# A selective scan with channels on partitions and its states in turn

## The chip, the cores and the metric

The kernel runs on one core of a Trainium2 chip. The metric is the device time in microseconds of one execution: the median of three runs before the change is 840.94 us (840.87 to 842.92). Engines are named as in the profile: PE (TensorE, matrix products), PEld (its weight loads), DVE (VectorE), ACT (ScalarE), POOL (GpSimd) and SP (SyncE, which issues all DMAs).

## What is computed

32 images are cut into 36 patches each and run through one tower layer: patch embedding, layer norm, a gated block with a selective scan, a feed-forward block, layer norm, and a mixture of 16 experts of which 4 are used per token. The change concerns the scan:

```python
dt_in, Bm, Cm = jnp.split(xdbl, [DT_RANK, DT_RANK + D_STATE], axis=-1)
dt = jax.nn.softplus(jnp.einsum('blr,dr->bld', dt_in, W_dt) + b_dt)
A = -jnp.exp(A_log)
A_bar = jnp.exp(dt[..., None] * A)
Bx = (dt * z)[..., None] * Bm[:, :, None, :]
_, h = jax.lax.associative_scan(comb, (A_bar, Bx), axis=1)   # h = A_bar * h + Bx
y = jnp.einsum('blds,bls->bld', h, Cm) + D_skip * z
```

d runs over 384 inner channels, s over 16 states, l over the 36 tokens of an image; A_log differs from channel to channel and from state to state. B and C (Bm, Cm) have one value per token and state, for all channels.

## The kernel before

The work is cut into 4 chunks of 8 images, T = 288 tokens in a row on the free axis. One list (`schedule()`, the ORDER) fixes the program order of every engine. Each chunk has phase A (embedding to feed-forward) and phase B (the experts). Phase A of chunk 0 runs alone, together with a prologue (`split_w1`, 16 times) that splits the expert weights into two float32r parts and stores them to DRAM. Then a loop of three passes runs phase A of chunk c interleaved with phase B of chunk c-1, and phase B of the last chunk ends the program. How many pieces of phase B stand ahead of a step of phase A is a table (PIECES_BEFORE for expert up projections, DOWNS_BEFORE for down projections, SPLIT_BEFORE for the prologue's splits).

In the scan a partition holds one pair of channel and state: 8 channels times 16 states make a group, 48 groups cover 384 channels, and a step takes two groups, 576 columns; 24 steps per chunk, 8 for each of three blocks of 128 channels. The values of a group come from the [channel, token] tiles through PE, as a float32r product with a 0/1 matrix (`pick_group`) that repeats each channel over 16 partitions. For that dt and u = dt*z are split into high and low halves first (`split`: ACT copies, DVE or POOL subtractions into `dt_rows`, `u_rows`). A step (`expand_u`, `expand_dt`, `drive`, `decay_step`, `advance`, `collect`) is:

- PE: two products of u_rows into the PSUM banks pb 0 and 1 (after DVE has read the last pair), two of dt_rows into pa 0 and 1 (after ACT has read them)
- DVE: `b_x` = B * u, 576 columns, out of PSUM (line 1013); ACT: `a_bar` = exp(decay * dt), two halves out of PSUM
- DVE: `tensor_tensor_scan` of `a_bar` and `b_x`, both in SBUF, into `state`, 576 columns (line 1022)
- POOL: `read` = state * C, 576 columns (line 1262); DVE does the last of the chunk (line 1029)
- PE: two f32 products of `read` with `sum_channel` (128 rows, 32 columns each) that add the 16 states of each channel in pa bank 2; after 8 steps DVE makes y (line 1037)

`state`, `a_bar` and `read` have two buffers, `b_x` three. The softplus of blocks 1 and 2 is done inside the scan: ACT `square`, then at steps 4 and 12 five dependent DVE instructions (`log1p`, lines 983 and 987), then `split` at steps 6 and 14. Fifteen down projections stand inside the scan of each pass of the loop, and no up projection does. Five splits of the prologue stand in the scan of chunk 0 or at its end, seven behind it.

## Time and profile before

The profiled execution took 842.2 us, of which the span of the core's instructions is 840.4 us.

| | |
|---|---|
| median of three runs | 840.94 us |
| profiled execution | 842.2 us |
| its span | 840.4 us |
| PE busy | 642.1 us (76%) |
| DVE busy | 557.6 us (66%) |
| POOL busy | 314.2 us (37%) |
| ACT busy | 268.3 us (32%) |
| mean granted TensorE clock | 0.83 |

The span is a start of 52.6 us, a scan of 86.0 us, and a tail of chunk 0 of 55.7 us; then three passes of the loop, each with a scan of about 79 us and about 112 us of other work; and a last stretch of experts. "Start to start" below is the difference of two rows' start times. An arrow gives the engine that ended a wait.

### The profile page before, as it was taken

The page shows a single profiled execution, that of the slowest core. Times are in us where ns is not written, and L with a number is a line of the kernel's source. Part 1 is how long each engine was busy: PE and PEld are TensorE (multiplying, and loading weights), DVE is VectorE, ACT ScalarE, POOL GpSimd, SP SyncE. Part 2 cuts the span into 40 slices and gives each one's busy share as a digit, 9 for nine tenths or more (in the row PEclk, how much of TensorE's full clock was granted, in tenths as well). Part 3 has the DMA queues.
Part 4 walks back from the last instruction along what each step waited for, and adds up shares of the span by engine and source line. Part 5 has one row for each costly group of instructions (what it writes and reads, how often), then busy time and mean ns, then how long its engine had stood idle before and what let it go on. Part 6 is the DMA issues. An engine that isn't in the chain of part 4 may idle for free.

```text
span 840.4 us, 10439 instructions
## 1 busy us (share of the span) xinstructions
PE 642.1 (76%) x2988; PEld 434.8 (52%) x2988; DVE 557.6 (66%) x944; ACT 268.3 (32%) x617; POOL 314.2 (37%) x283
## 2 busy tenths in 40 slices
PE   5636466768877758988877758989967758987986
PEld 4423233547643437856743427767743426856664
DVE  3268975244798885555698895554698894555464
ACT  1363341213634322212543322212544322222231
POOL 2535774532236542121236552131136552122222
PEclk8756766759976789979967689989977699986999
DMA  9830202553300003132300003132200003131340
GB/s 292 268 133 1 92 24 73 176 200 136 113 1 2 0 1 114 57 124 99 113 0 1 0 0 113 57 124 100 79 33 1 0 0 110 59 123 56 114 161 20
DMA packets 15138, 66.55 MB, mean 79 GB/s; under 512 B 2096, under 2 KB 7648, under 8 KB 9840
## 3 DMA queue, kind: packets, MB, share of 16 engines
q1 hardware_dynamic: 15088, 66.04, 23.0%
q14 instruction: 38, 0.31, 0.1%
q8 instruction: 12, 0.20, 0.1%
HBM read 55.71 MB, written 10.32 MB: 79 GB/s over the span
## 4 chain that ended last, share of the span: by engine, by line
PE 40%; issue 23%; POOL 15%; DVE 14%; ACT 5%; SPq 1%; DMA 1%; POOLq 1%; DVEq 0%; ACTq 0%
PE pa L487 21%; PE pb L487 19%; POOL read L1262 5%; POOL scratch L1275 4%; DVE state L1022 3%; POOL root L1206 2%; DVE dt L983 1%; ACT scratch L765 1%; DVE hid L1168 1%; DVE scratch L1151 1%; POOL u_rows L1243 1%; POOL u L1236 1%; POOL w L1222 1%; DVE scratch L1159 1%; DVE b_x L1013 1%
## 5 line engine op out<-in xcount | busy, mean ns | idle before, releaser
L1275 POOL TENSOR_TENSOR scratch<-scratch 128x288 f32<-128x288 f32 x96 | 77.4, 806 | 290.5 <-DVE scratch L1159 290.5
L1262 POOL TENSOR_TENSOR read<-state,c_all 128x576 f32<-128x576 f32 x92 | 135.9, 1481 | 118.0 <-DVE state L1022 116.2
L1022 DVE TENSOR_TENSOR_SCAN state<-a_bar,b_x 128x576 f32<-128x576 f32 x96 | 172.0, 1795 | 5.3 <-POOL read L1262 3.5
L487 PE MATMUL pb<-t_high,w 128*128 128x288 f32 x576 | 154.6, 333 | 9.4 <-DVE scratch L1143 6.3
L765 ACT ACTIVATE a_bar<-pa,decay 128x280 f32<-128x280 f32 x192 | 84.4, 490 | 155.0 <-PE pa L487 82.0
L487 PE MATMUL pb<-u_rows,pick_group 128*128 128x288 f32 x192 | 69.6, 454 | 73.4 <-DVE b_x L1013 57.2
L487 PEld LDWEIGHTS pb<-t_high,w 128*128 128x128 f32 x576 | 104.0, 198 | 30.8 <-DVE scratch L1143 11.3
L487 PE MATMUL pb<-hid,w 128*64 128x288 f32 (+1 forms) x384 | 106.5, 480 | 17.4 <-DVE hid L1168 17.4
L487 PE MATMUL pa<-read,sum_channel 128*32 128x288 f32 x384 | 85.3, 544 | 36.3 <-POOL read L1262 24.8
L487 PE MATMUL pb<-t_low,w 128*128 128x288 f32 x384 | 111.0, 303 | 0.0
L765 ACT ACTIVATE scratch<-pb,vec 128x288 f32<-128x288 f32 x96 | 48.0, 500 | 179.9 <-PE pb L487 179.8
L487 PEld LDWEIGHTS pb<-u_rows,pick_group 128*128 128x128 f32 x192 | 40.8, 255 | 124.5 <-DVE b_x L1013 90.8
L1013 DVE TENSOR_TENSOR b_x<-b_all,pb 128x576 f32<-128x576 f32 x96 | 70.9, 739 | 23.8 <-PE pb L487 23.5
L487 PEld LDWEIGHTS pb<-hid,w 128*64 128x64 f32 (+1 forms) x384 | 46.3, 179 | 61.1 <-issue 35.8
L487 PEld LDWEIGHTS pb<-t_low,w 128*128 128x128 f32 x384 | 75.3, 196 | 0.0
L1143 DVE TENSOR_SCALAR scratch<-pb,vec 128x288 f32<-128x288 f32 x96 | 49.4, 514 | 37.2 <-PE pb L487 36.6
L487 PE MATMUL pa<-dt_rows,pick_group 128*128 128x288 f32 x192 | 56.6, 385 | 7.2 <-ACT a_bar L765 7.2
L1168 DVE TENSOR_TENSOR hid<-scratch,pb 128x288 f32<-128x288 f32 x96 | 43.2, 450 | 22.1 <-POOL scratch L1275 22.1
L487 PEld LDWEIGHTS pa<-dt_rows,pick_group 128*128 128x128 f32 x192 | 43.6, 260 | 10.7 <-ACT a_bar L765 10.2
L487 PEld LDWEIGHTS pa<-read,sum_channel 128*32 128x32 f32 x384 | 16.2, 125 | 62.3 <-POOL read L1262 33.3
L765 ACT ACTIVATE scratch<-scratch 128x288 f32<-128x288 f32 x96 | 41.8, 436 | 14.4 <-DVE scratch L1143 14.3
L1159 DVE SCALAR_TENSOR_TENSOR scratch<-scratch 128x288 f32<-128x288 f32 x96 | 43.7, 456 | 0.9
(146 smaller groups left out, 859.5 us busy)
## 6 DMA issues: line engine op xcount, KB each, us to landing
w<-w_store SPq DMA_DIRECT2D x32, 1152.0 KB, 5.1
w_store<-w SPq DMA_DIRECT2D x8, 1152.0 KB, 5.0
scratch<-expert_w SPq DMA_DIRECT2D x16, 384.0 KB, 5.6
x_patch<-patches SPq DMA_DIRECT2D x4, 864.0 KB, 4.6
w<-expert_w SPq DMA_DIRECT2D x1, 2304.0 KB, 13.5
x_patch<-patches SPq DMA_DIRECT2D x3, 288.0 KB, 4.2
w_embed<-embed_w SPq DMA_DIRECT2D x3, 256.0 KB, 3.7
out_main<-result SPq DMA_DIRECT2D x4, 144.0 KB, 2.2
```

Of the source, the lines that this page charges most:

```text
L487: return nc.tensor.matmul(out, lhsT, rhs, start=start, stop=stop)
L765: return nc.scalar.activation(out, in_, func, **kw)
L983: dve.scalar_tensor_tensor(dt[:, j, :], factors[:, k, :], rest, product, ALU.add, ALU.mult).then_inc(poly.sem, 1)
L1013: dve.tensor_tensor(b_x[:, i % 3, :].rearrange("p (k t) -> p k t", k=2), twice(b_all[:, :]), pb[:, 0:2, 0:T], ALU.mult).then_inc(bx_ready. ...
L1022: dve.tensor_tensor_scan(state[:, i % 2, :], a_bar[:, i % 2, :], b_x[:, i % 3, :], 0.0, ALU.mult, ALU.add).then_inc(scanned.sem, 1)
L1143: dve.tensor_scalar(g_min[un % 2], pb[:, GATE, 0:T], col("b1_gate", un), LIMIT, ALU.add, ALU.min)\
L1151: dve.tensor_scalar(l_clip[un % 2], l_raw[un % 2], 1.0 + LIMIT, 1.0 - LIMIT, ALU.min, ALU.max)\
L1159: dve.scalar_tensor_tensor(g_act, g_tanh, 1.0, g_min[un % 2], ALU.add, ALU.mult)\
L1168: dve.tensor_tensor(hid[:, un % HID_TILES, :], glu, pb[:, WEIGHT, 0:T], ALU.mult)\
L1206: pool.tensor_tensor(root[:, 1, :], root[:, 0, :], minus_half[:, :], ALU.pow)\
L1262: pool.tensor_tensor(read[:, i % 2, :].rearrange("p (k t) -> p k t", k=2), state[:, i % 2, :].rearrange("p (k t) -> p k t", k=2), twice(c_ ...
L1275: pool.tensor_tensor(glu, g_act, l_clip[un % 2], ALU.mult).then_inc(glu_ready.sem, 1)
```

## The change

In the new scan a partition is a channel. A half step g handles one block of 128 channels and one state, 288 columns; two halves are a step, so there are again 24 steps and 48 halves per chunk.

- B is not kept: for each half PE spreads one row of `bc_parts` over all 128 partitions into pa bank 0 or 1 (`spread`, one float32r product whose weights are one column of `pick_state` repeated), as soon as the scan two halves earlier is done. DVE multiplies it by u in place in PSUM (`fill`), and the scan reads a_bar from SBUF and b_x from PSUM (`advance`).
- C is spread once per chunk: 16 products and 16 ACT copies into `c_all` (16 x 288 columns), in `broadcast`, which now follows `log1p` of block 0.
- a_bar comes from `dt` in SBUF directly, with a decay per partition; no splits, no `dt_rows`, `u_rows`, `pick_group`. POOL makes u of blocks 1 and 2 (`drive_u`).
- The states are added by two f32 products of `read` with the 128x128 identity into pa bank 2, over a whole block.
- `decay` needs another layout: it is turned by a DMA of single elements into DRAM (`decay_rows`) and loaded from there; ACT waits for this load first of all. The loads of group_pick and channel_sum are gone.
- Buffers: a_bar 4 halves, state 3, read 3. The three ACT copies of pick_unit in chunk 0 become one, at `outproj`. Ten prologue splits stand in the scan of chunk 0, three behind it.
- Down projections stand one ahead of each collect; as before fifteen of them come to stand in the scan. Eleven expert units stand ahead of the scan, as before.

```diff
+HALVES = 2 * SCAN_STEPS
+A_SLOTS, STATE_SLOTS, READ_SLOTS = 4, 3, 3
...
-    pre += [("xproj", 0), ("delta", 0), ("broadcast", 0)]
-    pre += [("square", k) for k in range(FACTORS)] + [("log1p", 0), ("split", 0)]
+    pre += [("xproj", 0), ("delta", 0)] + [("square", k) for k in range(FACTORS)]
+    pre += [("log1p", 0), ("broadcast", 0)]
...
-                scan.append(("split", j + 1))
-        scan += [("scan", i), ("decay", i)]
-        if i >= 1:
-            scan.append(("advance", i - 1))
-        if i >= 3:
-            scan.append(("collect", i - 3))
-    scan += [("collect", SCAN_STEPS - 3), ("advance", SCAN_STEPS - 1), ("collect", SCAN_STEPS - 2),
-             ("collect", SCAN_STEPS - 1)]
+                scan.append(("drive_u", j + 1))
+        scan.append(("decay", i))
+        for g in (2 * i, 2 * i + 1):
+            scan += [("fill", g), ("advance", g)]
+        scan.append(("read", i))
+        if i >= 2:
+            scan.append(("collect", i - 2))
+    scan += [("collect", SCAN_STEPS - 2), ("collect", SCAN_STEPS - 1)]
...
-DOWNS_BEFORE = {("scan", 3): 1, ("scan", 4): 2, ("scan", 5): 1, ("scan", 6): 1, ("scan", 8): 2,
-                ("scan", 9): 1, ("scan", 12): 1, ("scan", 13): 3, ("scan", 17): 1, ("scan", 18): 1,
-                ("scan", 19): 1, ("scan", 20): 2, ("scan", 23): 1}
...
-SPLIT_BEFORE = [("inproj", 1), ("inproj", 2), ("xproj", 0), ("delta", 0), ("scan", 1), ("scan", 11),
-                ("scan", 13), ("scan", 19), ("outproj", 0), ("scale2", 0), ("ffn", 0), ("ffn", 1),
-                ("down", 0), ("center3", 0), ("variance3", 0), ("scale3", 0)]
...
+DOWNS_BEFORE = {("collect", i): 1 for i in range(1, 22)}
+SPLIT_BEFORE = [("inproj", 1), ("inproj", 2), ("xproj", 0), *(("decay", 2 * n + 2) for n in range(10)),
+                ("variance2", 0), ("ffn", 0), ("ffn", 1)]
...
+            sp.dma_start(decay_rows, decay_log.rearrange("p g -> g p"), allow_slow_non_contiguous=True)\
+                .then_inc(decay_turned.sem, 16)
...
+            sp.wait_ge(decay_turned.sem, 16)
+            sp.dma_start(decay[:, :, :], decay_rows.rearrange("(j a) (b n) -> (a b) j n", j=NJ, n=STATES))\
+                .then_inc(load_decay.sem, 16)
...
+            def spread(bank, which, n):
+                pick = pick_state[:, which, n:n + 1].to_broadcast([P, P])
+                return mm(pa[:, bank, 0:T], pick, bc_parts[:, :], True, True)
...
-                for k in range(2):
-                    pe.wait_ge(v_max.sem, v_max.at(c, k + 1))
-                    mm(pa[:, 1 + k, 0:T], pick_state[:, k, :], bc_parts[:, :], True, True).then_inc(pe_bc.sem, 1)
...
-            def expand_u(c, i):
-                j = i // STEPS_PER_BLOCK
-                if i:
-                    pe.wait_ge(bx_ready.sem, bx_ready.at(c, i))
...
-                for k in range(2):
-                    _, q, b = scan_slot(i, k)
-                    last = mm(pb[:, k, 0:T], pick_group[:, 4 * (b % 2) + q, :], u_rows[:, j, b // 2, :], True, True)
-                last.then_inc(pe_u_all.sem, 1)
-            def expand_dt(c, i):
...
-                    mm(pa[:, k, 0:T], pick_group[:, 4 * (b % 2) + q, :], dt_rows[:, j, b // 2, :],
-                       True, True).then_inc(pe_dt_all.sem, 1)
+                for n in range(STATES):
+                    if n < NJ:
+                        pe.wait_ge(v_max.sem, v_max.at(c, n + 1))
+                    else:
+                        pe.wait_ge(c_ready.sem, c_ready.at(c, n - NJ + 1))
+                    spread((n + 1) % NJ, 1, n).then_inc(pe_c.sem, 1)
+            def fill(c, g):
+                if g < 2:
+                    pe.wait_ge(c_ready.sem, c_ready.at(c, STATES))
+                else:
+                    pe.wait_ge(scanned.sem, scanned.at(c, g - 1))
+                spread(g % 2, 0, g % STATES).then_inc(pe_b.sem, 1)
...
                 for k in range(2):
-                    _, q, b = scan_slot(i, k)
-                    last = mm(pa[32 * b:32 * b + 32, 2, 0:T], sum_channel[:, q, :],
-                              read[:, i % 2, k * T:(k + 1) * T], q == 0, q == 3)
+                    last = mm(pa[:, 2, 0:T], ident[:, :], read[:, i % READ_SLOTS, k * T:(k + 1) * T],
+                              r == 0 and k == 0, r == STEPS_PER_BLOCK - 1 and k == 1)
...
-                for k, tile in enumerate((b_all, c_all)):
-                    act.wait_ge(pe_bc.sem, pe_bc.at(c, k + 1))
-                    activate(tile[:, :], pa[:, 1 + k, 0:T], ACT.Copy).then_inc(bc_ready.sem, 1)
-            def split(c, j):
-                act.wait_ge(poly.sem, poly.at(c, POLY_STEPS * (j + 1)))
-                activate(dt_rows[0:P // 2, j, 0, :], dt[0:P // 2, j, :], ACT.Copy)
...
+                for n in range(STATES):
+                    act.wait_ge(pe_c.sem, pe_c.at(c, n + 1))
+                    activate(c_all[:, n, :], pa[:, (n + 1) % NJ, 0:T], ACT.Copy).then_inc(c_ready.sem, 1)
...
-                    for k in range(3):
-                        rounded = activate(pick_unit[0:MIX_ROWS, 8 * k:8 * (k + 1), :], raw_unit[k], ACT.Copy)
...
-                if i >= 2:
-                    act.wait_ge(scanned.sem, scanned.at(c, i - 1))
-                for k in range(2):
-                    j, q, b = scan_slot(i, k)
-                    group = GROUPS_PER_BLOCK * j + 4 * b + q
-                    act.wait_ge(pe_dt_all.sem, pe_dt_all.at(c, 2 * i + k + 1))
-                    activate(over_images(a_bar[:, i % 2, k * T:(k + 1) * T]), over_images(pa[:, k, 0:T]), ACT.Exp,
-                             scale=decay[:, group:group + 1]).then_inc(decayed.sem, 1)
+                if i % STEPS_PER_BLOCK == 0:
+                    act.wait_ge(poly.sem, poly.at(c, POLY_STEPS * (i // STEPS_PER_BLOCK + 1)))
+                for g in (2 * i, 2 * i + 1):
+                    j, n, _, a = scan_half(g)
+                    if g >= A_SLOTS:
+                        act.wait_ge(scanned.sem, scanned.at(c, g - A_SLOTS + 1))
+                    activate(over_images(a), over_images(dt[:, j, :]), ACT.Exp, scale=decay[:, j, n:n + 1])\
+                        .then_inc(decayed.sem, 1)
...
+            def outproj(c, _):
...
+                    activate(pick_unit[0:MIX_ROWS, :, :], raw_unit, ACT.Copy).then_inc(picks_rounded.sem, 1)
...
-            act.wait_ge(load_ssm.sem, 16 * len(SSM_LOADS))
-            activate(decay[:, :], decay[:, :], ACT.Exp).then_inc(decay_exp.sem, 1)
+            act.wait_ge(load_decay.sem, 16)
+            activate(decay[:, :, :], decay[:, :, :], ACT.Exp).then_inc(decay_exp.sem, 1)
...
-            def split(c, j):
-                dve.wait_ge(dt_high.sem, dt_high.at(c, j + 1))
-                dve.tensor_tensor(dt_rows[P // 2:P, j, 0, :], dt[0:P // 2, j, :],
-                                  dt_rows[0:P // 2, j, 0, :].bitcast(F32), ALU.subtract)
...
-            def drive(c, i):
-                if i == 0:
...
-                dve.wait_ge(pe_u_all.sem, pe_u_all.at(c, i + 1))
-                dve.tensor_tensor(b_x[:, i % 3, :].rearrange("p (k t) -> p k t", k=2), twice(b_all[:, :]),
-                                  pb[:, 0:2, 0:T], ALU.mult).then_inc(bx_ready.sem, 1)
-            def advance(c, i):
...
-                if i >= 2:
-                    dve.wait_ge(read_out.sem, read_out.at(c, i - 1))
-                dve.tensor_tensor_scan(state[:, i % 2, :], a_bar[:, i % 2, :], b_x[:, i % 3, :], 0.0,
-                                       ALU.mult, ALU.add).then_inc(scanned.sem, 1)
+            def fill(c, g):
+                j, n, b_x, _ = scan_half(g)
+                if n == 0:
+                    dve.wait_ge(u_ready.sem, u_ready.at(c, j + 1))
+                dve.wait_ge(pe_b.sem, pe_b.at(c, g + 1))
+                dve.tensor_tensor(b_x, u[:, j, :], b_x, ALU.mult).then_inc(bx_ready.sem, 1)
+            def advance(c, g):
+                _, _, b_x, a = scan_half(g)
+                dve.wait_ge(decayed.sem, decayed.at(c, g + 1))
+                if g % 2 == 0 and g >= 2 * STATE_SLOTS:
+                    dve.wait_ge(read_out.sem, read_out.at(c, g // 2 - STATE_SLOTS + 1))
+                dve.wait_ge(bx_ready.sem, bx_ready.at(c, g + 1))
+                dve.tensor_tensor_scan(state_half(g), a, b_x, 0.0, ALU.mult, ALU.add).then_inc(scanned.sem, 1)
...
-            def split(c, j):
...
+            def drive_u(c, j):
...
                 pool.wait_ge(poly.sem, poly.at(c, POLY_STEPS * (j + 1)))
                 pool.tensor_tensor(u[:, j, :], dt[:, j, :], z[:, j, :], ALU.mult).then_inc(u_ready.sem, 1)
-                pool.wait_ge(u_ready.sem, u_ready.at(c, j + 1))
-                pool.wait_ge(u_high.sem, u_high.at(c, j + 1))
-                pool.tensor_tensor(u_rows[P // 2:P, j, 0, :], u[0:P // 2, j, :],
-                                   u_rows[0:P // 2, j, 0, :].bitcast(F32), ALU.subtract).then_inc(u_low.sem, 1)
...
-            def advance(c, i):
+            def read_states(c, i):
...
-                pool.wait_ge(scanned.sem, scanned.at(c, i + 1))
...
+                if i < STEPS_PER_BLOCK:
+                    pool.wait_ge(c_ready.sem, c_ready.at(c, 2 * i + 2))
+                pool.wait_ge(scanned.sem, scanned.at(c, 2 * i + 2))
+                if i >= READ_SLOTS:
+                    pool.wait_ge(pe_y.sem, pe_y.at(c, i - READ_SLOTS + 1))
+                pool.tensor_tensor(read[:, i % READ_SLOTS, :], state[:, i % STATE_SLOTS, :], c_pair(i), ALU.mult)\
+                    .then_inc(read_out.sem, 1)
```

PE in the first block of the scan of chunk 0, before; `u_rows` and `dt_rows` are the split halves, `read` the states times C:

```order
51 L487 MATMUL pb<-u_rows,pick_group 128x288 [waits bx_ready]
52 L487 MATMUL pb<-u_rows,pick_group 128x288
53 L487 MATMUL pa<-dt_rows,pick_group 128x288 [waits decayed] x2
54 L487 MATMUL pa<-read,sum_channel 32x288 [waits read_out]
55 L487 MATMUL pa<-read,sum_channel 32x288
```


and now, where `bc_parts` holds B and C and `pick_state` picks a row:

```order
40 L487 MATMUL pa<-bc_parts,pick_state 128x288 [waits scanned] x2
41 L487 MATMUL pa<-read,ident 128x288 [waits read_out]
42 L487 MATMUL pa<-read,ident 128x288
43 L487 MATMUL pa<-bc_parts,pick_state 128x288 [waits scanned] x2
44 L487 MATMUL pa<-read,ident 128x288 [waits read_out]
45 L487 MATMUL pa<-read,ident 128x288
```


Four products that feed a step are two now, each waits for a scan, and the sum over states has 128 columns of weights in place of 32.

DVE in the same scan, before:

```order
65 L1013 TENSOR_TENSOR b_x<-b_all,pb 128x576 [waits pe_u_all,scanned]
66 L1022 SCALAR_TENSOR_TENSOR state<-a_bar,b_x 128x576 [waits read_out,bx_ready,decayed]
67 L1013 TENSOR_TENSOR b_x<-b_all,pb 128x576 [waits pe_u_all,scanned]
68 L1022 SCALAR_TENSOR_TENSOR state<-a_bar,b_x 128x576 [waits read_out,bx_ready,decayed]
69 L1013 TENSOR_TENSOR b_x<-b_all,pb 128x576 [waits pe_u_all,scanned]
```


and now, where `pa` as an input and output is B and then b_x in PSUM:

```order
33 L966 TENSOR_TENSOR pa<-u,pa 128x288 [waits pe_b]
34 L975 SCALAR_TENSOR_TENSOR state<-a_bar,pa 128x288 [waits bx_ready,decayed]
35 L966 TENSOR_TENSOR pa<-u,pa 128x288 [waits pe_b]
36 L975 SCALAR_TENSOR_TENSOR state<-a_bar,pa 128x288 [waits bx_ready,read_out,decayed]
37 L966 TENSOR_TENSOR pa<-u,pa 128x288 [waits pe_b]
38 L975 SCALAR_TENSOR_TENSOR state<-a_bar,pa 128x288 [waits bx_ready,decayed]
```


A step of two instructions became one of four of half the width, and each scan waits for the fill right ahead of it.

SP at the start, before:

```order
13 L473 DMA result<-state_pick 64x256
14 L473 DMA w_dt<-dt_w 96x384
15 L473 DMA decay<-decay_log 128x48
16 L473 DMA hid<-group_pick 128x1024
17 L473 DMA sum_channel<-channel_sum 128x128
18 L422 DMA scratch<-expert_w 128x2x384 x3
19 L478 DMA w_out<-out_w 128x768 [waits constants]
```


and now:

```order
9 L466 DMA ident<-identity 128x128
10 L467 DMA decay_rows<-decay_log 6144x1x1
11 L470 DMA w_in<-in_w 128x768
12 L470 DMA w_in_rest<-in_w_rest 64x768
13 L470 DMA w_xproj<-xproj_w 128x384
14 L470 DMA result<-state_pick 64x256
15 L470 DMA w_dt<-dt_w 96x384
16 L417 DMA scratch<-expert_w 128x2x384 x3
17 L475 DMA decay<-decay_rows 128x3x16 [waits decay_turned,constants]
18 L478 DMA w_out<-out_w 128x768
```


The turning DMA of 6144 single elements stands ahead of the weights, the load of decay behind the raw expert weights, and SP waits for the first before it issues the second.

## Rows read from the trace of the kernel before

**Rows 1.** Windows by stage: busy us of each engine, then clock, DMA share, GB/s.

```profile
core 0: us, PE busy (x) PEld busy (x) DVE busy (x) ACT busy (x) POOL busy (x), PEclk, DMA share, GB/s
...
52.60:138.60 86.00, 50.56 (x190) 24.16 (x188) 73.64 (x66) 31.35 (x73) 58.25 (x39) 0.64 0.14 46
138.60:194.30 55.70, 40.63 (x137) 28.81 (x137) 15.98 (x45) 11.41 (x26) 19.34 (x19) 0.70 0.47 165
...
233.60:312.80 79.20, 56.34 (x232) 28.32 (x232) 70.71 (x67) 27.33 (x63) 42.32 (x30) 0.76 0.00 1
```

**Rows 2.** Groups by form, VectorE: count, busy us, mean ns, idle before.

```profile
L1022 DVE TENSOR_TENSOR_SCAN state<-a_bar,b_x 128x576 f32<-128x576 f32 x96 | 172.0, 1795 | 5.3 <-POOL read L1262 3.5 <-ACT a_bar L765 1.8
...
L1013 DVE TENSOR_TENSOR b_x<-b_all,pb 128x576 f32<-128x576 f32 x96 | 70.9, 739 | 23.8 <-PE pb L487 23.5
...
L1168 DVE TENSOR_TENSOR hid<-scratch,pb 128x288 f32<-128x288 f32 x96 | 43.2, 450 | 22.1 <-POOL scratch L1275 22.1
...
L998 DVE TENSOR_TENSOR dt_rows<-dt,dt_rows 64x288 fp32r<-64x288 f32 x12 | 15.4, 1284 | 0.2
...
L991 DVE TENSOR_TENSOR u<-dt,z 128x288 f32<-128x288 f32 x4 | 1.8, 458 | 0.1
```

**Rows 3.** Timeline of one scan step at full clock: start us, us, engine, line.

```profile
299.79 0.72 DVE L1013 TENSOR_TENSOR b_x<-b_all,pb 128x576 f32<-128x576 f32 x1
299.95 1.42 POOL L1262 TENSOR_TENSOR read<-state,c_all 128x576 f32<-128x576 f32 x1 [1.29 <-DVE state L1022]
...
300.44 2.15 DVE L1022 TENSOR_TENSOR_SCAN state<-a_bar,b_x 128x576 f32<-128x576 f32 x1
...
300.57 0.53 PE L487 MATMUL pb<-u_rows,pick_group 128*128 128x288 f32 x2 [1.18 <-DVE b_x L1013]
...
301.42 0.68 PE L487 MATMUL pa<-read,sum_channel 128*32 128x288 f32 x4
...
302.51 0.72 DVE L1013 TENSOR_TENSOR b_x<-b_all,pb 128x576 f32<-128x576 f32 x1
```

**Rows 4.** Timeline, a scan with POOL not reading, second channel block.

```profile
253.53 1.35 DVE L1022 TENSOR_TENSOR_SCAN state<-a_bar,b_x 128x576 f32<-128x576 f32 x1
```

**Rows 5.** Timeline of a step at half clock with a down projection in it.

```profile
286.51 1.18 PE L487 MATMUL pa<-read,sum_channel 128*32 128x288 f32 x4 [0.30 <-POOL read L1262]
...
287.62 1.33 PE L487 MATMUL pb<-hid,w 128*128 128x288 f32 x2
...
289.46 0.76 DVE L1013 TENSOR_TENSOR b_x<-b_all,pb 128x576 f32<-128x576 f32 x1 [0.43 <-PE pb L487]
```

**Rows 6.** Timeline, 128-column f32 matmuls at full clock, ahead of the second scan.

```profile
209.60 0.65 PE L487 MATMUL pa<-squares,w_in 128*128 128x288 f32 x2
...
210.09 0.65 PE L487 MATMUL pa<-squares,w_in_rest 128*128 128x288 f32 x2
```

**Rows 7.** Timeline, the same matmuls at half clock, first chunk.

```profile
30.05 1.17 PE L487 MATMUL pa<-squares,w_in 128*128 128x288 f32 x2
...
31.01 1.02 PE L487 MATMUL pa<-squares,w_in_rest 128*128 128x288 f32 x2
```

**Rows 8.** Timeline, VectorE polynomial of the second block inside the scan.

```profile
243.12 2.52 DVE L983 SCALAR_TENSOR_TENSOR dt<-ffn,dt 128x288 f32<-128x288 f32 x3
```

**Rows 9.** Timeline, ScalarE copies of B and C ahead of the scan.

```profile
222.38 0.39 ACT L765 ACTIVATE b_all<-pa 128x288 f32<-128x288 f32 x1
...
222.67 0.40 ACT L765 ACTIVATE c_all<-pa 128x288 f32<-128x288 f32 x1
```

**Rows 10.** Timeline, ScalarE in the first chunk: its first work, one pick copy.

```profile
14.20 0.24 ACT L765 ACTIVATE decay<-decay 128x48 f32<-128x48 f32 x1 [12.17 <-DMA sum_channel<-channel_sum]
...
46.80 1.05 ACT L765 ACTIVATE pick_unit<-state 48x1024 fp32r<-48x1024 f32 x1
```

**Rows 11.** DMA queue between 6.5 and 8.2 us.

```profile
DMA packets 614, 0.59 MB, mean 349 GB/s; under 512 B 198, under 2 KB 451, under 8 KB 614
...
q1 hardware_dynamic: 614, 0.59, 106.1%
```

164 lines of the change are left out of this document (52 added, 112 removed).

## Prediction, made before the changed kernel was run

> **What bounds the kernel now.** I read the stages first, then the scan step by step. A scan of a loop pass takes 79.2 us, and DVE is busy in 70.7 of them, PE in 56.3, ACT in 27.3 and POOL in 42.3 [rows 1]; the scan of chunk 0 takes 86.0 us, with DVE busy in 73.6. So in the scan the chain runs through DVE. The groups say that DVE is not busy with work alone: the scan instruction has a mean of 1795 ns [rows 2], while it takes 1.35 us where POOL does not read at that time [rows 4]. The timeline of a step shows why. POOL starts its read (1.42 us) at 299.95, when a scan has ended; DVE does b_x (0.72 us), starts its next scan at 300.44, and that scan lasts 2.15 us [rows 3]. It ends 1.22 us after POOL's read does, nearly the time it takes alone: it stood still meanwhile. The product that takes one input from PSUM lasts 0.72 us with POOL reading beside it, the same as its mean of 739 ns [rows 2, 3]. Two SBUF inputs on DVE wait for POOL; one SBUF and one PSUM input do not. A step is 2.72 us, from 299.79 to 302.51 [rows 3], and only 0.65 + 1.28 = 1.93 of it is DVE's own work.
>
> **The step of the new scan.** A half is a fill and a scan of 288 columns. The fill: no row shows DVE writing to PSUM. The nearest are 0.450 us (one PSUM input, SBUF output) and 0.458 (all SBUF) [rows 2]; I take 0.46, bounds 0.40 and 0.52. The scan: a product grows from 0.45 to 0.74 us between 288 and 576 columns [rows 2], 0.16 us fixed and 1.0 ns per column; a scan of 1.35 us [rows 4] is then 0.16 fixed and 2.07 ns per column, so 0.76 for 288, bounds 0.68 (half of 1.35) and 0.84. DVE starts its next instruction 0.07 us before the last ends when it need not wait for it (0.72 long, 0.65 apart [rows 3]); that holds from scan to fill and not from fill to scan. A half is 0.46 + 0.76 - 0.07 = 1.15 us, a step 2.30. This is more DVE work than before (1.93), but the scan now has one SBUF input, so the 0.8 us of standing still goes: 2.30 against 2.72.
>
> What is late next? POOL needs 1.42 per step and has no wait for DVE's inputs left; hidden. ACT needs two exponentials, some 0.9 us, from SBUF, four halves ahead; hidden. PE is close. Full clock: two spreads (two float32r products took 0.53 [rows 3]), the sum of two f32 products with 128 columns, each 0.49 start to start [rows 6], and a down projection, 0.49: 2.0 us, under 2.30. The old sum took 0.68 [rows 3]; the 0.3 more is hidden there. Half clock: an f32 product is 0.96 [rows 7], so 0.5 to 0.85 + 1.92 = 2.4 to 2.8 us without a down projection and 3.4 to 3.7 with one. Then the two spreads, which stand behind sum and down projection in PE's order, are late and DVE waits for B. Price: 1.2 us for each step with a down projection at half clock. The clock was 0.76 in the loop's scans [rows 1] and PE has more columns per us to stream now, so I take 4 or 5 of the 15 such steps at half clock: 5.5 us; bounds 0 and 15 us.
>
> **One scan of the loop.** 48 halves x 1.15 = 55.2. Two polynomials stay: 2.52 us for the three middle instructions, one of which waits for POOL's read [rows 8], + 2 x 0.46 + 0.25 = 3.7 each, 7.4. Two y at 0.48, 0.9. The end (last read, product, y): 3.0. Sum 66.5, with PE's lateness 72.0. Before 79.2 less 0.2 for the shorter ones: -7 us. The splits (L998 alone 15.4 us in the program [rows 2]) are gone and are in this sum.
>
> **Ahead of a loop scan.** C costs 16 copies where B and C took two, 0.29 us apart [rows 9]: 14 x 0.3 = 4.2 us more on ACT. They stand behind two expert units and ahead of one, and the first fill waits for all 16, so they are not hidden: DVE and PE have little else then. Behind them the last unit's products and copies add about 1 us. What goes is the split of block 0, four DVE instructions and four copies, some 2 us of the path. Net +3, bounds +1 and +5. The down projections in the scan are fifteen before and after: 0.
>
> **Chunk 0.** No down projections: a step is set by PE at half clock (2.4 to 2.8) or by POOL (1.42 and half of a weight split of 2.2 us); ten splits stand here now instead of four. I take 2.6: 62.4 + 7.4 + 0.9 + 3.4 + 2 (splits that the polynomial waits for) = 76, against 86.0 [rows 1]: -10. Ahead of it three pick copies of 1.05 us [rows 10] move to `outproj`, where ACT waits for PE anyway, and the split goes, C comes: -2. Behind it, five fewer splits in the 55.7 us [rows 1]: -3.
>
> **The start.** ACT's first work starts at 14.20, 12.17 us after it began to wait for the first loads [rows 10]. Now it waits for two DMAs in a row, the first of 6144 elements, 384 for each of 16 DMA engines. Between 6.5 and 8.2 us, 614 packets filled the 16 engines [rows 11]: 1.7 x 16 / 614 = 44 ns each, with nearly 1 KB in the mean. So the turning costs between 0 and 384 x 47 ns = 18 us (47 with the queue's 106%); I take the middle, 9. The weights and the raw expert weights are queued behind it, and the load of decay behind those. The first weights were there at 14.2; I estimate 15.5 for the raw weights behind them, less the loads that are gone, so decay lands at 15.5 + 9 + 2 = 26.5: +12.5 us, bounds +3.5 and +21.5. Nothing covers it; every later step of chunk 0 hangs on ACT's first.
> A rule that speaks against this: the Trainium skill, "DMA: Bandwidth & Descriptors" (Rules for kernel authors), says that a non-contiguous last dimension becomes one descriptor per element, and "VectorE: DVE Perf Modes" (The three transpose paths) puts a strided transposing copy of 128x128 at 19 times 1309 ns. That would be 1.5 ns per element, an estimate of 9.3 us for 6144, inside my bounds; no run here shows it yet.
>
> **The sum** against the profiled execution's 842.2 us: loop 3 x (-7 + 3) = -12; chunk 0 -10 - 2 - 3 = -15; start +12.5. Together -14.5: 827.7. The median lies 1.3 below the profiled execution: 826.4, written as 826.5.
>
> **Rivals.** (1) *PE keeps its clock*: the scans cost 66.5, 3 x -5.5 = -16.5 more: 810. For it: at 299 to 303 us PE was at full clock with only some 1.6 us of work a step. Against: 0.76 in the mean. (2) *PE at half clock sets the step* (slower than before): 12 of the 15 down steps at 3.5 us: 14.5 us a scan in place of 5.5, +27: 853. It turns slower once about 9 of the 15 are at half clock. For it: the step that starts at 285.76 already waited 0.43 for PE behind a sum and a down projection [rows 5]; the sum is 0.8 us longer now. (3) *PSUM operands cost DVE extra* (slower): the upper bounds 0.52 and 0.84 make a half 1.29, 192 x 0.14 = +27: 853. Against it: 0.450 and 0.458 hardly differ [rows 2].
> On (3) the Trainium skill speaks against the change: "VectorE: DVE Perf Modes" (The TRN2 errata — SBUF-src ops pay a fixed extra latency per instruction) gives 58 cycles fixed for an SBUF source and 120 for PSUM. By that each of the 384 instructions would cost 65 ns more, an estimate of +25 us, 851; the row of 0.450 does not bear it out.
> (4) *The turning costs more than its bound*: at 90 ns an element it is 35 us, 26 more, 852; four-byte writes to DRAM are not in the trace. (5) *The scan still waits for POOL*, so that the change doesn't do what it says: up to 0.8 a step, 75 us, far above all. Against it: the product with a PSUM input beside POOL's read [rows 3].
>
> **How the numbers follow.** Forecast (815 to 838) 0.42; rival 1 0.18; rival 2 0.14; rival 3 0.12; rival 4 0.07; rival 5 0.02; other mixtures near the old time 0.05. The range reaches from rival 1 to the lower part of rivals 2 to 4: 805 to 852. The least that a measurement can tell from no change is about 0.3%, 2.5 us. Faster is the forecast, rival 1 and a little: 0.62. Within 0.3%: 0.11. Slower: rivals 2 to 5 and a little, 0.27.
>
> **What would show it.** In the profile after: a fill near 0.46 and a scan near 0.76 us, no longer when POOL reads; steps of 2.30 us without a down projection; DVE waiting for PE's spread only at half clock; loop scans of 72 us; 16 C copies some 0.3 us apart; ACT's first work at 26.5 us. I am wrong if scans show two lengths, if a fill is over 0.5, if ACT starts after 36, or if DVE waits for PE at full clock.

## The result: slower, by the one DMA at the start

The changed kernel takes 851.87 us in the median of four runs (848.39 to 857.17), the kernel before in the same session 841.01 (840.87 to 842.92): a ratio of 1.013, 95% interval 1.0105 to 1.0154. The forecast was 826.5 us, so it had the wrong sign; the measured time lies where its rivals 2 to 4 stood, at the upper end of its range. Runs that came out over 1.5% above the fastest run of the same kernel are slow ones, and every median, range and ratio below leaves them out. The profiled execution took 850.91 us with a span of 848.8 (before 842.2 and 840.4). The mean granted clock of TensorE rose from 0.827 to 0.865.

I read the stages first. Windows of the changed kernel: start:end, length, busy us of each engine with its count of instructions, then clock, DMA share, GB/s. The borders are ACT's first work, the first fill of a scan and the end of its last y.

```profile
core 0: us, PE busy (x) PEld busy (x) DVE busy (x) ACT busy (x) POOL busy (x), PEclk, DMA share, GB/s
0.00:51.30 51.30, 8.49 (x24) 6.00 (x24) 7.47 (x8) 1.29 (x2) 5.05 (x19) 0.66 1.34 90
51.30:88.40 37.10, 25.64 (x74) 16.73 (x74) 9.81 (x22) 16.29 (x43) 8.86 (x9) 0.68 0.68 200
88.40:162.80 74.40, 48.81 (x143) 30.37 (x142) 64.78 (x110) 38.64 (x78) 56.64 (x48) 0.80 0.41 135
162.80:256.90 94.10, 72.55 (x331) 56.32 (x331) 42.60 (x109) 29.41 (x72) 17.66 (x18) 0.85 0.26 96
256.90:329.80 72.90, 53.41 (x188) 33.47 (x189) 62.68 (x111) 27.45 (x55) 34.76 (x26) 0.88 0.00 1
329.80:444.90 115.10, 101.66 (x527) 80.53 (x526) 63.51 (x166) 38.63 (x94) 23.95 (x27) 0.93 0.26 93
```

The scan of chunk 0 takes 74.4 us (86.0 in [rows 1]) and the loop's first scan 72.9 (79.2); the other two take 72.9 and 73.8. In place of 70.7 us, DVE is busy for 62.7. But the first row has 51.3 us in which next to nothing is computed. Against the kernel before, the span splits up like this:

| stretch | forecast | measured |
|---|---|---|
| start, to ACT's first work | +12.5 | +37.1 (51.3 against 14.2) |
| chunk 0: ahead of, in and behind the scan | -2, -10, -3 | -1.3, -11.6, -5.7 |
| three scans of the loop | -21 | -17.1 |
| the rest of the loop and the last stretch | +9 | +7.0 |
| sum | -14.5 | +8.4 |

Without the start it is -28.7 us where the forecast had -27. The whole miss is in one row. "Behind" is counted from the last y of chunk 0's scan to the u of the next chunk (88.1 us before, 82.4 after), and the stretch from that u to the first fill is in the row of the rest. The chain of the changed kernel (start us, us, what) shows what fills it:

```profile
4.97 39.03 DMA decay_rows<-decay_log
44.08 7.19 DMA decay<-decay_rows
```

The timeline of ACT (idle time before an instruction, and what ended it, in brackets) has its first work behind it:

```profile
51.29 0.24 ACT L744 ACTIVATE decay<-decay 128x48 f32<-128x48 f32 x1 [49.27 <-DMA decay<-decay_rows]
```

In [rows 10] that was 14.20. The turning of 6144 elements took 39.0 us and not 9; with 384 elements on each of 16 DMA engines that is 102 ns for one, as a mean of the whole DMA. It is no steady pace: 2595 packets of under 512 bytes fall between 7 and 9 us, 737 between 9 and 13, none between 30 and 35, and the DMA lands at 44.0. The embedding (L751) stands behind this instruction in ACT's order, and all of chunk 0 behind that.

The queue suffered too. The timeline of SP's issues (start us, us that the issue took) shows the load of w_in, right behind the turning, held up for 14.89 us, where the loads just ahead of it took 0.4 and the two just behind it 0.5 to 0.6:

```profile
4.97 0.71 SPq L467 DMA_DIRECT2D decay_rows<-decay_log  x1
5.72 14.89 SPq L470 DMA_DIRECT2D w_in<-in_w  x1
20.66 0.54 SPq L470 DMA_DIRECT2D w_in_rest<-in_w_rest  x1
```

The scan itself reads as forecast, but for one term, the gap between a fill and its scan. First the groups of the changed kernel (count, busy us, mean ns, idle time before): the scan is short and has one length, and POOL's read is little changed (1481 ns before).

```profile
L1204 POOL TENSOR_TENSOR read<-state,c_all 128x576 f32<-128x576 f32 x92 | 129.7, 1412 | 130.5 <-DVE state L975 122.9
...
L975 DVE TENSOR_TENSOR_SCAN state<-a_bar,pa 128x288 f32<-128x288 f32 x192 | 144.7, 753 | 21.8 <-DVE pa L966 1.4
...
L966 DVE TENSOR_TENSOR pa<-u,pa 128x288 f32<-128x288 f32 x192 | 85.3, 444 | 16.5 <-PE pa L487 16.4
```

Then one step on the timeline of the changed kernel, DVE and POOL:

```profile
312.20 1.40 POOL L1204 TENSOR_TENSOR read<-state,c_all 128x576 f32<-128x576 f32 x1 [1.02 <-DVE state L975]
312.37 0.45 DVE L966 TENSOR_TENSOR pa<-u,pa 128x288 f32<-128x288 f32 x1
...
312.92 0.75 DVE L975 TENSOR_TENSOR_SCAN state<-a_bar,pa 128x288 f32<-128x288 f32 x1
313.59 0.44 DVE L966 TENSOR_TENSOR pa<-u,pa 128x288 f32<-128x288 f32 x1
...
314.14 0.75 DVE L975 TENSOR_TENSOR_SCAN state<-a_bar,pa 128x288 f32<-128x288 f32 x1
314.81 0.44 DVE L966 TENSOR_TENSOR pa<-u,pa 128x288 f32<-128x288 f32 x1
```

POOL reads from 312.20 to 313.60 and the scan at 312.92 takes its 0.75 us all the same: the 2.15 us of [rows 3] are gone. A step, though, is 2.44 us (312.37 to 314.81) and not 2.30. From fill to scan it is 0.55 us with a fill of 0.45: the scan starts 0.10 us after the fill has ended. Where DVE need not wait for its own result, from scan to fill, it starts 0.08 before.

### The profile page after: what moved, and what is told of

Read it like the earlier page. It is cut to its first block, busy times and chain, and to the rows that moved or that the text cites. A ratio compares the mean times of both kernels' runs of the same rounds, so it can differ in the third digit from the quotient of the medians.

```text
span 848.8 us, 10285 instructions
## 1 busy us (share of the span) xinstructions
PE 644.6 (76%) x2852; PEld 466.5 (55%) x2852; DVE 515.6 (61%) x1104; ACT 280.9 (33%) x623; POOL 274.1 (32%) x266
## 2 busy tenths in 40 slices
DMA packets 21137, 65.96 MB, mean 78 GB/s; under 512 B 8448, under 2 KB 13872, under 8 KB 15792
## 4 chain that ended last, share of the span: by engine, by line
PE 44%; DVE 25%; issue 14%; ACT 6%; DMA 5%; POOL 4%; DVEq 1%; SPq 0%; POOLq 0%; ACTq 0%
PE pa L487 25%; PE pb L487 19%; DVE state L975 7%; DVE pa L966 7%; DMA decay_rows<-decay_log 5%; DVE dt L951 4%; POOL scratch L1216 2%; ACT a_bar L744 2%; POOL root L1159 2%; ACT scratch L744 1%; DVE scratch L1104 1%; DMA decay<-decay_rows 1%; DVE scratch L1096 1%; ACT ffn L744 1%; ACT sp_exp L744 1%
## 5 line engine op out<-in xcount | busy, mean ns | idle before, releaser
L487 PE MATMUL pa<-bc_parts,pick_state 128*128 128x288 f32 x256 | 110.2, 477 | 88.8 <-DVE state L975 82.9
L975 DVE TENSOR_TENSOR_SCAN state<-a_bar,pa 128x288 f32<-128x288 f32 x192 | 144.7, 753 | 21.8 <-DVE pa L966 1.4
L744 ACT ACTIVATE a_bar<-dt,decay 128x280 f32<-128x280 f32 x192 | 100.4, 527 | 148.3 <-DVE state L975 148.2
L487 PEld LDWEIGHTS pa<-bc_parts,pick_state 128*128 128x128 f32 x256 | 57.7, 229 | 139.4 <-DVE state L975 122.9
L487 PE MATMUL pa<-read,ident 128*128 128x288 f32 x384 | 129.6, 466 | 3.4 <-DVE read L983 2.3
L744 ACT ACTIVATE scratch<-pb,vec 128x288 f32<-128x288 f32 x96 | 48.1, 501 | 180.8 <-PE pb L487 180.8
L487 PE MATMUL pb<-hid,w 128*64 128x288 f32 (+1 forms) x384 | 98.9, 453 | 10.6 <-DVE hid L1121 10.6
L487 PEld LDWEIGHTS pa<-read,ident 128*128 128x128 f32 x384 | 78.8, 218 | 34.8 <-issue 6.5
L966 DVE TENSOR_TENSOR pa<-u,pa 128x288 f32<-128x288 f32 x192 | 85.3, 444 | 16.5 <-PE pa L487 16.4
L1096 DVE TENSOR_SCALAR scratch<-pb,vec 128x288 f32<-128x288 f32 x96 | 49.3, 513 | 49.4 <-PE pb L487 48.6
L744 ACT ACTIVATE scratch<-scratch 128x288 f32<-128x288 f32 x96 | 41.8, 435 | 12.6 <-DVE scratch L1096 12.5
L1104 DVE TENSOR_SCALAR scratch<-scratch 128x288 f32<-128x288 f32 x96 | 29.3, 306 | 21.2 <-ACT scratch L744 21.1
L487 PE MATMUL pa<-h,mean_ones 128*128 128x288 f32 x16 | 6.3, 475 | 42.4 <-ACT h L744 40.7
## 6 DMA issues: line engine op xcount, KB each, us to landing
w<-expert_w SPq DMA_DIRECT2D x1, 2304.0 KB, 14.5
```

The costliest lines, as they stand in the source:

```text
L487: return nc.tensor.matmul(out, lhsT, rhs, start=start, stop=stop)
L744: return nc.scalar.activation(out, in_, func, **kw)
L966: dve.tensor_tensor(b_x, u[:, j, :], b_x, ALU.mult).then_inc(bx_ready.sem, 1)
L975: dve.tensor_tensor_scan(state_half(g), a, b_x, 0.0, ALU.mult, ALU.add).then_inc(scanned.sem, 1)
L1096: dve.tensor_scalar(g_min[un % 2], pb[:, GATE, 0:T], col("b1_gate", un), LIMIT, ALU.add, ALU.min)\
L1104: dve.tensor_scalar(l_clip[un % 2], l_raw[un % 2], 1.0 + LIMIT, 1.0 - LIMIT, ALU.min, ALU.max)\
```

## Experiments on the start

The theory after the first look: the turning alone costs the 37 us, it does so in front of any kernel, and its price is one of 4-byte writes to DRAM. The rival: the late start was partly covered, or the price is one of the number of elements alone.

**Layout by the host.** The array is handed over as decay wants it, and one plain load stands in the place of the turning.

```diff
-            sp.dma_start(decay_rows, decay_log.rearrange("p g -> g p"), allow_slow_non_contiguous=True)\
-                .then_inc(decay_turned.sem, 16)
+            sp.dma_start(decay[:, :, :], decay_log).then_inc(load_decay.sem, 16)
...
-    a["decay_log"] = i["L0_attn_A_log"].reshape(NJ * GROUPS_PER_BLOCK, P).T
+    a["decay_log"] = i["L0_attn_A_log"].reshape(NJ, P, STATES).transpose(1, 0, 2)
```

> The changed kernel, with decay_log handed over in the layout of decay ([128, 3, 16]) and loaded in the place of the turning DMA; decay_rows, the turning and the second load are gone, all else stays. Theory (the turning is the whole loss): ACT's first work at 13 to 15 us as before the change (14.20) in place of 51.3, the time falls by 37 us, to 813 to 817, faster than before by 3 to 3.4%. Rival (ACT's late start was partly covered, other loads are late anyway): the time falls by less than 30 us, to over 822, and chunk 0 waits elsewhere. In both, the loop's scans stay at 72.9 us.

Measured: 813.71 us (812.35 to 816.37), 0.967 of the time before, 0.963 to 0.970. ACT's first work is at 9.03 us, earlier than the 13 to 15 that were expected, since decay now lands ahead of the other weights. Its embedding starts at 11.92 (14.34 before the change); the scans of the loop take 73.4 to 73.8. The theory holds: the turning is the loss. The kernel is 27.8 us faster than the one before, and not all of that is the scan: its first fill comes at 46.7 us against 52.6, and only 1.3 of these 5.9 us were gained between ACT's first work and the scan in the changed kernel. I estimate the earlier start at the other 4.6.

**The turning in front of the old kernel.** The same DMA is put ahead of the old kernel's weights, and its load of decay waits for it.

```diff
+            sp.dma_start(decay_rows, decay_log.rearrange("p g -> g p"), allow_slow_non_contiguous=True)\
+                .then_inc(decay_turned.sem, 16)
             for dst, src in SSM_LOADS:
...
+            sp.wait_ge(decay_turned.sem, 16)
+            sp.dma_start(decay[:, :], decay_log).then_inc(load_decay.sem, 16)
```

> The kernel before, with the turning DMA issued ahead of the weights and its own load of decay behind it, for which ACT waits as the changed kernel does; the scan and all else are the old ones, and what the turning writes is not read. Theory (the start alone costs 37 us, whatever kernel follows): ACT's first work at 50 to 52 us, 841 + 37 = 876 to 880 us. Rival (in the kernel before, the old weight splits and longer chunk 0 cover part): 850 to 870.

Measured: 877.95 us (876.21 to 879.70), ratio 1.042, 1.038 to 1.046. That is +36.4 us, with ACT's first work at 50.73 (+36.5); the turning took 36.3 us here and the load behind it 9.4. Nothing in either kernel covers the start.

**Writes apart.** The same elements from DRAM to DRAM, walked the other way round: the writes now lie 512 bytes apart.

```diff
-            sp.dma_start(decay_rows, decay_log.rearrange("p g -> g p"), allow_slow_non_contiguous=True)\
+            sp.dma_start(decay_rows.rearrange("g p -> p g"), decay_log, allow_slow_non_contiguous=True)\
```

> The changed kernel with the same turn of 6144 elements from DRAM to DRAM, but walked the other way: the reads follow each other in memory and the writes lie 512 bytes apart, where they followed each other before. Theory A (the dear part is that 4-byte writes to neighbouring addresses of DRAM follow each other): the DMA lands within 10 to 15 us, ACT's first work at 22 to 30 us, the time is 822 to 832. Theory B (any 4-byte write to DRAM is dear): it stays at about 39 us, ACT at 48 to 54 us, 848 to 856.

Measured: 825.89 us (823.11 to 828.67), ratio 0.981, 0.977 to 0.985. The chain of this kernel:

```profile
5.05 15.50 DMA decay_rows<-decay_log
20.63 7.98 DMA decay<-decay_rows
```

15.5 us in place of 39.0 with as many elements and as many bytes: 40 ns for one, and inside the prediction's bounds of 0 and 18. It landed 0.5 us above the 15.0 that theory A allowed; B is out. Both kernels have the same number of packets on their pages, 21137, of which 8448 are under 512 bytes, so the other walk did not save any; they go faster. The kernel with the host's layout has 14721, which is 6416 fewer: about one packet for each of the 6144 elements. DMA view of 9 to 13 us, the changed kernel and then this one:

```profile
DMA packets 737, 0.00 MB, mean 1 GB/s; under 512 B 737, under 2 KB 737, under 8 KB 737
...
DMA packets 2638, 0.01 MB, mean 3 GB/s; under 512 B 2638, under 2 KB 2638, under 8 KB 2638
```

So the price is not that of 4-byte writes to DRAM as such. The edit changes the reads as well: they lay 192 bytes apart and now follow each other. That the reads were the dear part is settled by the next kernel, which reads 192 bytes apart and is faster still. What is left is that the writes follow each other at neighbouring addresses; the walk also deals the elements to the engines in another way, and no run separates that.

The Trainium skill, "DMA: Bandwidth & Descriptors" (Specifications), says that below 512 bytes a DMA engine reads, changes and writes back. Both kernels write 4 bytes at a time, so by itself this doesn't separate 40 ns from 102. That neighbouring writes wait for each other there is a reading that fits and is not shown: no run here looks into the memory.

**Straight into SBUF.** Three DMAs bring the elements one by one from decay_log to decay.

```diff
+            for j in range(NJ):
+                sp.dma_start(decay[:, j, :], decay_log[:, j * 16:(j + 1) * 16]
+                             .rearrange("(b n) a -> a b n", n=STATES), allow_slow_non_contiguous=True)\
+                    .then_inc(load_decay.sem, 16)
...
```

> The changed kernel, but the 6144 elements go one by one from decay_log straight into decay in SBUF, three DMAs of 2048; the array in DRAM between and the second load are gone. Theory A (an element costs 102 ns wherever it is written): the DMAs end at about 44 us as the turning did, the second load's 7 us go, ACT starts at 44 to 46 us, the time is 844 to 847. Theory B (the write of 4 bytes to DRAM is the dear part, and into SBUF an element costs at most the 44 ns of the packets of the old start): 17 us or less, ACT starts at 22 to 26 us, the time is 822 to 828.

Measured: 807.77 us (two runs, 807.50 and 808.03), ratio 0.959, 0.956 to 0.962, below what either theory gave. SP's issues of this kernel:

```profile
5.16 5.18 SPq L466 DMA_DIRECT2D decay<-decay_log  x3
10.38 1.39 SPq L470 DMA_DIRECT2D w_in<-in_w  x1
```

ACT's first work is at 13.94 us. From 5.16 to 13.91 all 6144 elements were in SBUF: 8.75 us, 23 ns for one of 384. Theory B was right in kind and too dear by half. That this kernel beats the host's layout by 6 us although ACT starts 4.9 us later is not the start: its stretches between scans had a higher granted clock (behind chunk 0's scan 0.89 against 0.86 and 80.5 us against 82.4, the next 0.98 against 0.95 and 99.7 against 102.1). Why the clock differed I did not look into.

**Fewer elements.** Only 24, then 16, then 32 of the 48 rows are turned; the others arrive in rows and are copied whole. The cut shows the kernel with 16.

```diff
+            part = 16
+            sp.dma_start(decay_rows[0:part, :], decay_log.rearrange("p g -> g p"), allow_slow_non_contiguous=True)\
+                .then_inc(decay_turned.sem, 16)
+            sp.dma_start(decay_rows[part:48, :], decay_rest).then_inc(decay_turned.sem, 16)
...
```

> The changed kernel, but only 24 of the 48 rows (3072 of 6144 elements) are turned by the DMA; the other 24 come in rows and are copied whole. Theory (a price for each element, 102 ns on each of 16 engines): the turning takes 192 x 102 ns = 19.6 us, ACT's first work comes at 31 to 33 us, the time is 831 to 835. Rival (a fixed cost of such a DMA, or of one in front of the loads): the turning still takes over 30 us, ACT starts after 42 us, the time is 843 to 853.

> As e4_half_turned, but with 16 of the 48 rows turned (2048 elements). e4 took 30.3 us for 24 rows against 39.0 for 48, which is neither a price per element (19.6) nor no price. Theory A (a DMA engine works through whole rows, and the engine with the most rows sets the end: 3 for 48 rows, 2 for 24, 1 for 16; then a row is 8.7 us and 13 us are fixed): 16 rows take 21 to 22 us. Theory B (a fixed cost and a price per element, 21.6 + 0.36 a row): 27 us. Theory C (13 us for each row of the fullest engine, with something else in e4's 30.3): 13 to 15 us. The time is 827 to 832, 841 to 845 or 820 to 825.

> As e4_half_turned, but with 32 of the 48 rows turned (4096 elements). Theory A (whole rows on an engine, two on each for 24 as for 32): 30 to 31 us as e4, the time 846 to 850. Theory B (a fixed cost and a price per element): 33 us, 849 to 853. Theory C: 26 to 30 us, 843 to 849.

Measured: 847.99 us with 24 rows (847.44 to 848.85), 827.73 with 16 (two runs, 823.85 and 831.62) and 841.29 with 32 (four runs, 833.48 to 842.63). The profile with 32 rows is of a longer run, 851.94 us. With 24 rows the profile gives the wait for both DMAs, 30.3 us, and not the landing of the turning alone. With 16 and 32 rows it gives it. DMA issues of the kernel with 16 rows (KB, us from issue to landing):

```profile
decay_rows<-decay_log SPq DMA_DIRECT2D x1, 8.0 KB, 13.5
decay_rows<-decay_rest SPq DMA_DIRECT2D x1, 16.0 KB, 15.8
```

The same of the kernel with 32 rows:

```profile
decay_rows<-decay_log SPq DMA_DIRECT2D x1, 16.0 KB, 24.4
decay_rows<-decay_rest SPq DMA_DIRECT2D x1, 8.0 KB, 32.4
```

So 16, 32 and 48 rows land after 13.5, 24.4 and 39.0 us, one, two and three rows for each of 16 engines: some 13 us for a row of 128 elements, 95 to 105 ns for an element, and next to no fixed part. Theories A (21 to 22 us with 16 rows) and B (27) are out. C gave 13 to 15 with 16 rows, which is met, and 26 to 30 with 32, where 24.4 is 1.6 us less; neither total time is in its range, 827.7 against 820 to 825 and 841.3 against 843 to 849. One profile of each is all there is, and 48 rows alone took 36.3, 39.0 and, further down, 49.4 us. What e4 added on top is the whole-row copy behind the turning, which landed 3 us after it with 16 rows and 9 with 32; both must land before decay is loaded. The Trainium skill, "DMA: Bandwidth & Descriptors" (Why a DMA increments its semaphore by 16 and not by 1), says that a DMA takes the largest number of engines up to 16 that divides its outermost dimension; for 24 rows that would be 12 engines with two rows each, as many as with 32. The waits for both DMAs, 30.3 us with 24 rows and 33.2 with 32, are in keeping with it and no proof.

**The turning behind all loads.** It is issued last, and decay is loaded and prepared where chunk 0 spreads C.

```diff
+            sp.dma_start(decay_rows, decay_log.rearrange("p g -> g p"), allow_slow_non_contiguous=True)\
+                .then_inc(decay_turned.sem, 16)
...
+            def log1p(c, j):
+                if not after_first(c) and j == 0:
+                    sp.wait_ge(decay_turned.sem, 16)
+                    sp.dma_start(decay[:, :, :], decay_rows.rearrange("(j a) (b n) -> (a b) j n", j=NJ, n=STATES))\
+                        .then_inc(load_decay.sem, 16)
...
```

> The changed kernel with the turning DMA behind all loads of the program (it is issued at about 16 us) and decay loaded, exponentiated and negated at chunk 0's broadcast, the first place near the first use. Theory A (it occupies the DMA engines and its own result only): the embedding and the projections start at 9 to 12 us, the turning lands at 16 + 39 = 55 us and the load of decay at about 60, where the broadcast at 40 us waits for it: 20 us late, 830 to 838. Theory B (whatever stands behind it in the queue crawls too, here the raw expert weights of the splits): the broadcast and the splits are later still, 840 to 855. Theory C (with no other transfers around it, the turning takes some 20 us): 815 to 822.

Measured: 832.43 us (five runs, 830.08 to 838.64), ratio 0.991, 0.988 to 0.994. The profile is of a longer run, 844.97 us, and has the chain

```profile
15.13 49.44 DMA decay_rows<-decay_log
64.59 5.31 DMA decay<-decay_rows
```

and SP's timeline shows the load of the next patches, behind the turning, held up in its issue for 30.5 us:

```profile
15.81 30.50 SPq L443 DMA_DIRECT2D x_patch<-patches  x1
```

The first fill comes at 76.8 us, 32.4 us after u (5.2 in the changed kernel). The median lies where theory A put it, but A had the turning at 39 us and it took 49.4 in the profiled run, whose time is one of B's; C is out. Why it took 10 us more here is open. Moved out of the way the DMA still costs 19 us (832.4 against 813.7 with the host's layout) of the 38 that it costs at the start: it has to be made cheap, not hidden.

## Experiments on the scan

All of these stand on the kernel with the host's layout, 813.7 us.

**b_x in SBUF.** The product writes b_x to SBUF, so that the scan has two SBUF inputs again, as in the kernel before.

```diff
-                dve.tensor_tensor(b_x, u[:, j, :], b_x, ALU.mult).then_inc(bx_ready.sem, 1)
+                dve.tensor_tensor(b_sb[:, g % 2, :], u[:, j, :], b_x, ALU.mult).then_inc(bx_ready.sem, 1)
...
-                dve.tensor_tensor_scan(state_half(g), a, b_x, 0.0, ALU.mult, ALU.add).then_inc(scanned.sem, 1)
+                dve.tensor_tensor_scan(state_half(g), a, b_sb[:, g % 2, :], 0.0, ALU.mult, ALU.add).then_inc(scanned.sem, 1)
```

> On e1_host_layout (813.7 us, decay laid out by the host): the product writes b_x to a tile in SBUF instead of PSUM, so that the scan reads two SBUF inputs; the product still reads B from PSUM. Theory (two SBUF inputs make DVE wait while POOL reads): scans that meet POOL's read of 1.41 us get up to 0.9 us longer, so that scans show two lengths (0.75 and 1.2 to 1.7), a step grows by 0.5 to 1.1 us where it had 2.43, the time is 840 to 890. Rival (the standing still of the old scan had to do with 576 columns or the old order, not with where the inputs lie): scans stay at 0.75, 810 to 818.

Measured: 861.62 us (two runs, 857.68 and 865.56), ratio 1.024, 1.018 to 1.029. The loop's scans take 88.4 us. Timeline of this kernel, DVE's scans and POOL's read:

```profile
256.69 0.76 DVE L970 TENSOR_TENSOR_SCAN state<-a_bar,b_sb 128x288 f32<-128x288 f32 x1
...
257.61 1.41 POOL L1199 TENSOR_TENSOR read<-state,c_all 128x576 f32<-128x576 f32 x1 [0.77 <-DVE state L970]
257.90 1.73 DVE L970 TENSOR_TENSOR_SCAN state<-a_bar,b_sb 128x288 f32<-128x288 f32 x1
...
260.08 0.76 DVE L970 TENSOR_TENSOR_SCAN state<-a_bar,b_sb 128x288 f32<-128x288 f32 x1
```

The scans no longer have one length. Of the 192, 94 take 0.76 us, 54 take 1.6 to 1.8, and the others lie between; the mean is 1.111 us (0.753 in the changed kernel). The long one above ends 0.61 us after POOL's read, nearly the time it takes alone, as the old one did in [rows 3]. This is the mechanism that the change removes, and putting it back costs 48 us, more than the 27.8 that the kernel with the host's layout had gained; a scan without POOL beside it keeps its 0.76. The Trainium skill, "SBUF — State Buffer" (SBUF: two separate sides), calls the port pair that DVE and GpSimd share an exclusive lock, which DVE needs for an instruction with two SBUF inputs beside a GpSimd read: this trace agrees, with 1.73 against 0.76 us.

**Half of C.** Only 8 of the 16 rows are spread and copied; states 8 to 15 read those of 0 to 7, so that part of the result is not computed.

```diff
-                for n in range(STATES):
+                for n in range(C_KEPT):
                     act.wait_ge(pe_c.sem, pe_c.at(c, n + 1))
...
```

> On e1_host_layout: only 8 of the 16 rows of C are spread and copied ahead of a scan; states 8 to 15 read those of 0 to 7, so this part of the computation is left out. Theory (the 16 copies stand on the path): from the last u to the first fill it is 8 x 0.3 = 2.4 us less in each of the four chunks, 9 to 11 us in all, the time is 803 to 805. Rival (the expert units placed there, not the copies, set when the scan begins): less than 3 us in all, 811 to 814.

Measured: 800.56 us (798.71 to 803.79), ratio 0.952, 0.949 to 0.955: 13.1 us for 8 copies in four chunks, 0.41 us a copy, and 2.4 us below what the theory allowed. From u to the first fill it is 2.9 to 3.5 us less in every chunk, 12.4 in all or 0.39 a copy. The copies stand on the path, dearer than the 0.29 us apart of [rows 9]; the rival is out. Timeline of ACT in the changed kernel, where they take 0.33 each:

```profile
248.66 5.33 ACT L744 ACTIVATE c_all<-pa 128x288 f32<-128x288 f32 x16
```

**The old places of the weight splits.** In chunk 0 four splits stand in the scan and eight behind it, where the change has ten and three.

```diff
-SPLIT_BEFORE = [("inproj", 1), ("inproj", 2), ("xproj", 0), *(("decay", 2 * n + 2) for n in range(10)),
-                ("variance2", 0), ("ffn", 0), ("ffn", 1)]
+SPLIT_BEFORE = [("inproj", 1), ("inproj", 2), ("xproj", 0), ("delta", 0), ("decay", 1), ("decay", 11),
+                ("decay", 13), ("decay", 19), ("outproj", 0), ("scale2", 0), ("ffn", 0), ("ffn", 1),
+                ("down", 0), ("center3", 0), ("variance3", 0), ("scale3", 0)]
```

> On e1_host_layout (813.7 us): the weight splits of the program's start are placed as the kernel before has them, four in chunk 0's scan and eight behind it, in place of ten and three. Theory (the splits that left the stretch behind chunk 0's scan are why it is 5.7 us shorter than before the change, and the ten that came into the scan cost little there): behind the scan +5 to +6 us (82.4 to 88), the scan 74.2 down by 0 to 2, the time 816 to 820. Rival (that stretch is shorter for another reason): behind the scan within 2 us of 82.4, the time 812 to 815.

Measured: 815.95 us (two runs, 814.82 and 817.09). Behind chunk 0's scan it is 85.3 us against 82.4, in the scan 73.2 against 74.2. The splits explain 2.9 of the 5.7 us, as the forecast had it (3); neither expectation is met. The other 2.8 go with a higher granted clock: over the same stretch it was 0.81 in the kernel before (88.1 us) and is 0.86 in both kernels here. That the clock is their cause is not shown.

**Fill one half ahead.** A third bank for B (one of the experts' that is idle in the scan), and DVE does the fill of the next half between fill and scan of this one.

```diff
         for g in (2 * i, 2 * i + 1):
-            scan += [("fill", g), ("advance", g)]
+            scan.append(("fill", g))
+            if g:
+                scan.append(("advance", g - 1))
...
```

> On e1_host_layout: a third PSUM bank for B, and DVE does the fill of half g+1 between fill and scan of half g, so that no instruction of DVE waits for the one just ahead of it; the sums are collected one step later. Theory (a half is fill 0.44 + scan 0.75 + 0.02 because the scan waits for the end of its own fill, 0.1 us more than two independent instructions take): a step falls from 2.43 to 2.22 to 2.26 us, a loop scan by 4 to 5 us, the time to 794 to 799. Rival (PE's spread or the half clock sets the step): the step stays over 2.38, 808 to 816.

Measured: 765.55 us (764.06 to 769.47), ratio 0.909, 0.907 to 0.912. That is 48 us less, more than twice what the theory gave. Timeline of DVE in this kernel:

```profile
243.53 0.45 DVE L971 TENSOR_TENSOR pa<-u,pa 128x288 f32<-128x288 f32 x1
243.89 0.74 DVE L980 TENSOR_TENSOR_SCAN state<-a_bar,pb 128x288 f32<-128x288 f32 x1
244.56 0.44 DVE L971 TENSOR_TENSOR pa<-u,pa 128x288 f32<-128x288 f32 x1
...
244.90 0.74 DVE L980 TENSOR_TENSOR_SCAN state<-a_bar,pa 128x288 f32<-128x288 f32 x1
```

A fill takes 0.45 us and the next scan starts 0.34 to 0.36 after it; that was 0.55. The term missed in my theory: the next instruction not only doesn't wait the 0.10 us, it also starts 0.09 to 0.10 before the end of the one ahead. A half is 1.01 us (243.89 to 244.90) in place of 1.22; for 192 halves that is 40 us, and the four scans are 6.7, 10.7, 11.1 and 11.3 us shorter, 39.8 together. The profiled runs differ by 42.7 us in their spans, so 3 of that lie outside the scans, and the medians by 5 more. The edit brings a third bank as well, but DVE's waits for B did not shrink with it (19.7 us in all against 17.6): what is gained is the gap between fill and scan. The Trainium skill, "VectorE: DVE Perf Modes" (Rules for kernel authors), advises to count instructions and not semaphores in a row of dependent ones. Here the count is the same in both kernels, and another order, with the bank that it needs, is worth 5.9%.

**C inside the scan.** Two rows of C a step in its first eight steps, through two idle banks of the experts; the down projections move behind them.

```diff
         scan.append(("decay", i))
+        if i == 0:
+            scan.append(("spread_c", 0))
         for g in (2 * i, 2 * i + 1):
...
+            if g % 2 == 0 and i + 1 < STEPS_PER_BLOCK:
+                scan.append(("spread_c", i + 1))
...
```

> On e1_host_layout: the 16 rows of C are spread and copied inside the scan, two a step in its first eight steps, one step ahead of their read, through two PSUM banks of the experts that are idle there; the down projections move to the steps behind. Theory (s2 showed 3.1 us a chunk for 8 copies; ACT has 1.1 us of each 2.43 us step free and PE at full clock 0.9): from the last u to the first fill 5 to 6 us less in each chunk, the scans +0 to +1 us, the time 791 to 797. Rival (PE's two more products make the fills late, or the later down projections do): the scans grow by 4 us or more, 805 to 815.

Measured: 789.56 us (788.15 to 790.08), ratio 0.938, 0.936 to 0.940. The first fill comes 0.5 us after u in chunk 0 (5.2 before) and 6.2 to 7.9 in the loop (11.7 to 14.1); the loop's scans take 71.2 to 73.4 where they took 73.4 to 73.8, and chunk 0's takes 75.5 where it took 74.2. The copies have moved beside DVE's work, at no cost in the loop and at 1.3 us in chunk 0; the rival is out.

**Both.**

> Both p1_c_inside and p2_fill_ahead on e1_host_layout. Theory: the gains add, 20 + 20 = 40 us less than 813.7, 770 to 780. Rival (in the first eight steps PE has four spreads, a sum of 0.97 us and its waits to do in 2.24 us, and is late): some of p2's gain goes there, 780 to 792.

Measured: 745.88 us (744.72 to 750.33), ratio 0.888, 0.885 to 0.892: 11% faster than the kernel before and 12.4% faster than the changed one. The loop's scans take 61.0 to 62.1 us, at a clock of 0.92. The gains add (813.7 - 48.1 - 24.1 = 741.5, and 4 us of it are given back; the scan of chunk 0 takes 70.2 us where the fill ahead alone had 67.5). That the time is below the 770 of the theory is no finding of this run: its terms, 20 and 20, had been sized too low. Windows of this kernel, the first scan of the loop and the stretch behind it:

```profile
200.00:262.20 62.20, 52.02 (x203) 34.92 (x204) 57.24 (x110) 31.21 (x69) 34.53 (x26) 0.92 0.00 1
262.20:370.70 108.50, 95.66 (x512) 75.53 (x510) 63.39 (x164) 34.12 (x79) 24.02 (x28) 0.95 0.28 98
```

DVE is busy in 57.2 of the 62.2 us of a scan.

## Why the prediction was wrong, point by point

- **The start: wrong, and it decided the sign.** The step that failed is "1.7 x 16 / 614 = 44 ns each ... so the turning costs between 0 and 384 x 47 ns = 18 us". The rows [rows 11] hold packets of nearly 1 KB in the mean that are written to SBUF. The operation to be priced writes 4 bytes to DRAM, and the text says itself, under rival 4, that such writes are not in the trace. A bound from rows of another kind of transfer was used as an upper end. Measured: 102 ns an element as the kernel walks them, 40 walked the other way, 23 into SBUF; the last two would have kept the bound. The sign "if ACT starts after 36" came true, at 51.3. Rival 4 had a chance of 0.07 because that bound was trusted. Its mechanism is the right one; that its 852 us came out to the microsecond is in part luck. It had 35 us for the turning, which took 39.0, and 15.5 + 2 for the rest up to ACT's first work, where 12.3 were measured (7.2 of them the load behind the turning).
- The Trainium skill's "19 times" for a transposing copy ("VectorE: DVE Perf Modes", The three transpose paths) gave an estimate of 9.3 us for the turning. The page says it of a copy whose innermost step in the destination is large. In the turning as the kernel walks it that step is the smallest there is, and it took 39.0 us; with writes 512 bytes apart it was 15.5, and into SBUF 8.75. Here the small step was the dear one, and only the last figure is near the estimate.
- **No lock in the new scan: right.** Scans have one length, 0.753 us against 0.76 taken; the experiment with b_x in SBUF shows the mechanism, at up to 1.77. Rival 5 is out.
- **PSUM operands: right.** The fill from PSUM to PSUM is 444 ns against 0.46 taken. Rival 3 is out, and for these instructions so is the rule named beside it: the Trainium skill, "VectorE: DVE Perf Modes" (The TRN2 errata — SBUF-src ops pay a fixed extra latency per instruction), gives a PSUM source 120 fixed cycles and an SBUF source 58. The trace does not agree. With b_x written to SBUF the product takes 0.43 us, with PSUM 0.44; with all of it in SBUF, [rows 2], 0.458.
- **The half: mis-sized.** 1.15 us, "and not from fill to scan" with a gap of nothing. It is 1.22: the scan starts 0.10 us after its fill has ended. 48 x 0.07 = 3.4 us a scan.
- **PE's lateness: mis-sized the other way.** 5.5 us a scan were taken, DVE waited 3.1 for B in the loop's first scan. The clock there rose from 0.76 to 0.88; rival 1's condition came true by half. The waits stand where the forecast had them, at or near a clock of one half: over the stretches of 3.6 us that hold them or lead up to them the granted clock was 0.50 for the longest, 1.9 us, and 0.50 and 0.72 for the other two, 0.4 and 0.8 us. There are three and not 4 or 5. The waits of the changed kernel in 256.9 to 329.8 us (us in total, times, longest) have it:

```profile
DVE pa L966 <- PE pa L487: 3.1, 3, 1.9
```

With 48 x 1.22 = 58.6, 7.0 for the two polynomials (3.5 each, not 3.7), 1.0 for two y, 2.8 for the end, 3.1 and one wait of 0.5 for a fill the sum is 73.0, measured 72.9. That the forecast had 72.0 is luck: 3.4 us too little for the halves and 2.4 too much for PE nearly cancel.
- **C ahead of the scan: low, and something else left out.** +3 net, measured from u to the first fill +4.8, +5.9 and +7.2, 17.9 in all against 9. A copy costs some 0.4 us of the path and not 0.3. That the rest of the loop and the last stretch came out at +7.0 is luck: behind the loop's scans 10.9 us were gained that no term had. From the last y to the sum behind the output projection (L1042, now L995) it is 8.2 us in place of 12.1. There the first products of the experts took 0.45 us each and take 0.29, and down products of 1.24 and 0.71 us stood ahead of the projection that do not stand there now.
- **Chunk 0: right in size.** -10 for the scan (-11.6), -2 ahead (-1.3); behind it -3 (-5.7), of which the splits are 2.9. What sets the scan is not what was named, PE at half clock or POOL: the clock there was 0.80, DVE was busy in 64.8 of the 74.4 us, and it waited for PE for 6.0.

## What to carry to other kernels

In these runs a DMA of single elements was priced by where and in which order it writes: choose a walk with its writes apart, write to SBUF, or let the host lay the array out, and never bound it by the packets of another transfer. Two DVE inputs of which one lies in PSUM keep DVE and GpSimd apart; here that is worth up to 1.0 us for a scan that meets a read, and 0.36 in the mean of all scans. And a chain of dependent DVE instructions is worth interleaving with the next one: a bank more and another order gave more than the change did.

## What was new about the hardware

- In a DMA of single 4-byte elements that follow each other at neighbouring addresses of DRAM, one cost 94 to 105 ns on a DMA engine at the start of the program, and 129 ns where the DMA stood behind all loads (49.4 us for 384); with the writes 512 bytes apart it was 40 ns, and into SBUF 23.
- What stands behind such a DMA in SP's queue is held up in its issue: 14.9 us for w_in here, 8.4 us with the writes apart, 30.5 us where it stood behind all loads. With 16, 24 and 32 rows turned the next DMA was held up for 2.8, 9.9 and 15.2 us.
- DVE starts a scan 0.10 us after the fill that it reads has ended, but an independent one 0.09 us before the end of the fill ahead of it: 0.2 us for a dependency between neighbours.
